# Two switch-expert stages: choice, gathering and combination rewritten

## The reference

```python
grouped = x.reshape(b, s // 32, 32, d)               # 64 groups of 32 tokens
logits = einsum('bntd,des->bntes', grouped, Wc) + bc  # 32 x 4 = 128 experts
logits = logits + tie                                 # 0 to 1e-6 over the 32 tokens
perm = (logits == max(logits, over the 32 tokens))    # one token per group and expert
permuted = einsum('bntd,bntes->bnesd', grouped, perm)
inner = relu(einsum('bnesd,esdf->bnesf', permuted, W1) + b1)   # 128 -> 32 features
result = einsum('bnesf,esdf->bnesd', inner, W2) + b2           # 32 -> 128
out = einsum('bnesd,bntes->bntd', result, perm)
```

## Time and profile before

| | us |
|---|---|
| median of 3 runs | 2787.95 |
| range of the runs | 2787.81 to 2790.35 |
| profiled execution | 2791.28 |
| its span, first to last instruction | 2789.5 |
| first switch stage in it | 2375.9 to 2473.5 |
| second switch stage in it | 2681.8 to 2780.3 |

### The profile page before, as it was taken

The page is one execution under the profiler, slowest core; times in us unless marked ns, Lnnn a source line. Parts: engine busy times, 40 slices in busy tenths (PEclk is TensorE's granted clock), DMA queues, the critical chain, the costliest instruction groups (busy, mean ns, idle before and its releaser), DMA issues. The chain is left out here.

```text
span 2789.5 us, 42839 instructions
## 1 busy us (share of the span) xinstructions
PE 2246.0 (81%) x15196; PEld 1529.7 (55%) x15196; DVE 1768.2 (63%) x4423; ACT 1388.1 (50%) x3630; POOL 718.1 (26%) x472
## 2 busy tenths in 40 slices
PE   5888887987988797897555888777776988689977
PEld 4666664663654464564335776243423766466647
DVE  5555555875964794794655664338355999447863
ACT  3444444763864584683621224554554765316750
POOL 0000001641640461461022431000010878041000
PEclk8999999989999998999767989798987999778986
DMA  1000002000100210110102320000001221100010
GB/s 54 13 13 13 13 1 73 21 20 19 24 17 5 81 25 12 24 28 4 47 9 54 74 53 18 11 11 3 6 11 33 87 72 53 64 10 1 2 64 16
DMA packets 79044, 80.94 MB, mean 29 GB/s; under 512 B 28624, under 2 KB 63952, under 8 KB 77808
## 3 DMA queue, kind: packets, MB, share of 16 engines
q1 hardware_dynamic: 78832, 78.19, 9.8%
HBM read 53.94 MB, written 8.52 MB: 22 GB/s over the span
## 5 line engine op out<-in xcount | busy, mean ns | idle before, releaser
L1016 ACT ACTIVATE window_s<-window_s,window_soft 128x128 f32<-128x128 f32 x512 | 197.8, 394 | 5.0 <-DVE window_soft L1179 5.0
L1094 POOL TENSOR_TENSOR window_pa<-window_pa,window_pb 128x1024 f32<-128x1024 f32 x64 | 151.5, 2366 | 152.3 <-DVE window_pb L1161 152.3
L1086 POOL TENSOR_TENSOR window_s<-window_s,window_soft 128x512 f32<-128x512 f32 x128 | 133.0, 1040 | 218.6 <-DVE window_soft L1116 218.4
L1179 DVE CUSTOM_DVE_ANT_0 window_s<-ps,window_mask,window_nrn 128x128 f32<-128x128 f32 x512 | 148.7, 347 | 46.7 <-PE ps L861 29.9
L3129 DVE TENSOR_TENSOR_SCAN mamba_bx<-ps,mamba_ab 128x256 f32<-128x256 f32 x256 | 154.6, 670 | 18.9 <-PE ps L2915 18.9
L824 PE MATMUL ps<-window_wa,window_sh 128*128 128x512 f32 x256 | 132.4, 643 | 41.6 <-DVE window_pb L1161 28.9
L417 PE MATMUL ps<-linattn_h,linattn_wb 128*128 128x512 f32 x192 | 107.5, 647 | 55.2 <-ACT linattn_h L494 55.2
L3299 ACT ACTIVATE rope_p<-ps,rope_mx 128x128 f32<-128x128 f32 (+1 forms) x256 | 104.3, 419 | 53.1 <-DVE rope_mx L3353 53.1
L2912 PE MATMUL ps<-mamba_m,mamba_xt 128*128 128x129 f32 x512 | 102.8, 283 | 29.6 <-ACT mamba_m L2987 20.6
L582 POOL TENSOR_TENSOR linattn_y<-linattn_y,linattn_wa 128x512 f32<-128x512 f32 x24 | 28.3, 1179 | 374.6 <-DVE linattn_xn L621 374.6
L83 PE MATMUL ps<-x,consts 128*128 128x512 f32 x120 | 78.4, 814 | 46.1 <-PEq L53 40.5
(11 more groups left out here) (607 smaller groups left out, 6243.3 us busy)
## 6 DMA issues: line engine op xcount, KB each, us to landing
mamba_cbr<-mamba_c SPq DMA_DIRECT2D x32, 512.0 KB, 3.6
window_vs<-window_vt SPq DMA_DIRECT2D x64, 128.0 KB, 2.3
delta_xi<-delta_x SPq DMA_DIRECT2D x16, 512.0 KB, 5.1
switch_w<-in_switch_w SPq DMA_DIRECT2D x4, 2048.0 KB, 10.0
window_wa<-in_window_wa SPq DMA_DIRECT2D x4, 1152.0 KB, 6.8
linattn_wb<-in_linattn_wb SPq DMA_DIRECT2D x6, 513.0 KB, 3.6
window_wb<-in_window_wb SPq DMA_DIRECT2D x4, 537.5 KB, 7.7
window_sh<-y SPq DMA_DIRECT2D x16, 128.0 KB, 2.2
```

Of the source, the lines that this page charges most:

```text
L1016: a = nc.scalar.activation(s[:, k % 2, e, c, :], s[:, k % 2, e, c, :], ACT.Exp, scale=-1.0, bias=soft[:, k % 2, e, 1, c:c + 1], accum_out= ...
L1086: nc.gpsimd.tensor_tensor(s[:, k % 2, e], s[:, k % 2, e], soft[:, k % 2, e, 3, :].unsqueeze(2).to_broadcast([P, QC, P]), ALU.mult)\
L1094: nc.gpsimd.tensor_tensor(own, own, pb[:, :, :, :].rearrange("p a h d -> p (a h d)"), ALU.add)\
L1179: v = nc.vector.tensor_tensor_reduce(s[:, k % 2, e, c, :], K.ps[:, B_S + e, toks(c, P)], mask[:, k % 2, :], nrn[:, k % 4, h:h + 1], 3e38, ...
```

## The change

- Choice: logits of chunk j go to bank 4 + j, the transposes of x to bank j. ACT's bias step is gone; DVE's first operation reads the logits from PSUM and adds bias and tie in one pass. ACT, not DVE, copies the transposed choice to `perm_tm`, and PE begins to gather after two chunks are turned.
- Gathering: a unit is a chunk and one of two pairs of groups (`units`). Its 8 products (16 passes) write two banks, j and j + 4; ACT copies the one, DVE the other, each with its own semaphore. `z` is laid out as feature, group, expert.
- Experts: the moving operand becomes `z[:, :, 4q + r]`, with steps of 128 words. `res` is a view of the same memory in the old order.
- Combination: the transposes of one chunk use banks 0 to 3; the copies to `resm` add nothing and are shared between ACT and DVE. For each tile a product of `perm` (128 tokens, stationary) with b2 (128 columns, moving) starts the sum; then each group's 32 columns of `perm` are the stationary operand on one of four column parts, and `resm`, 128 columns, moves. The result is tokens by features; ACT copies it to SBUF (`y_tm`, the memory of h), PE transposes it back, and DVE adds it to x. PE works on the transposes of chunk j + 1 ahead of the products of chunk j.

```diff
-    z = st.sb("z", [P, ES, NG])
+    z = st.sb("z", [P, NG, ES])
-    res = z
+    res = z[:, :, :].rearrange("p g e -> p (g e)").rearrange("p (e g) -> p e g", g=NG)
+    units = [(0, 0), (1, 0), (0, 1), (2, 0), (1, 1), (3, 0), (2, 1), (3, 1)]
+    seen = {u: n + 1 for n, u in enumerate(units)}
+    def picked_to(j, g):
+        return z[:, :, :].rearrange("p (j t g) e -> p j g t e", j=NJ, g=4)[:, j, g]
...
 PE
+            def turn_chosen(j):
+                pe.wait_ge(st.chosen, j + 1)
+                pe.wait_ge(st.x_copied, j + 1)
+                for t in range(TPW):
+                    mm = nc.tensor.transpose(K.ps[:, j, toks(t, P)], perm[:, toks(TPW * j + t, P)], K.ident)
+                mm.then_inc(st.chosen_tm, 1)
+            def pick(j, u):
+                pe.wait_ge(st.chosen_copied, j + 1)
+                if u:
+                    pe.wait_ge(st.picked_act, seen[j, 0])
+                    pe.wait_ge(st.picked_dve, seen[j, 0])
+                for t in range(TPW):
+                    for e in range(2):
+                        g = 2 * u + e
+                        rows, tile = slice(32 * g, 32 * g + 32), toks(TPW * j + t, P)
+                        mm = nc.tensor.matmul(K.ps[:, j + 4 * e, toks(t, P)], h_tm[rows, tile], perm_tm[rows, tile],
+                                              start=True, stop=True)
+                mm.then_inc(st.picked, 1)
+            def combine(j):
+                bank = K.ps[:, 4 + j % 2, :]
+                if j >= 2:
+                    pe.wait_ge(st.y_copied, j - 1)
+                for t in range(TPW):
+                    nc.tensor.matmul(bank[:, toks(t, P)], perm[:, toks(TPW * j + t, P)], b2, start=(t == 0), stop=False,
+                                     skip_group_check=True)
+                pe.wait_ge(st.moved_act, 2 * (j + 1))
+                pe.wait_ge(st.moved_dve, 2 * (j + 1))
+                for t in range(TPW):
+                    for g in range(4):
+                        n = 4 * (TPW * j + t) + g
+                        mm = nc.tensor.matmul(K.ps[32 * g:32 * g + 32, 4 + j % 2, toks(t, P)], perm[:, toks(n, GT)],
+                                              resm[:, n, :], start=False, stop=True, skip_group_check=True)
+                mm.then_inc(st.y_ready, 1)
...
+            for j in range(NJ):
+                logits(j)
+                turn_x(j)
+            turn_chosen(0)
+            turn_chosen(1)
+            for n, (j, u) in enumerate(units):
+                pick(j, u)
+                if n in (1, 3):
+                    turn_chosen(2 + n // 2)
...
-                                          z[:, 4 * q + r, :], start=True, stop=True)
+                                          z[:, :, 4 * q + r], start=True, stop=True)
...
-            for j in range(NJ):
-                pe.wait_ge(st.result_ready, min(4 * j + 4 + 8, NT))
-                for g in range(16 * j, 16 * j + 16):
-                    mm = nc.tensor.matmul(K.ps[:, 4 + j, toks(g % 16, GT)], resm[:, g, :], perm[:, toks(g, GT)],
-                                          start=True, stop=True)
-                mm.then_inc(st.y_ready, 1)
+            turn_result(0)
+            for j in range(NJ):
+                if j + 1 < NJ:
+                    turn_result(j + 1)
+                combine(j)
+                if j:
+                    turn_back(j - 1)
+            turn_back(NJ - 1)
...
 ACT
+            turned_chosen(0)
+            turned_chosen(1)
+            for n, (j, u) in enumerate(units):
+                picked(j, u)
+                if n in (1, 3):
+                    turned_chosen(2 + n // 2)
...
+            for j in range(NJ):
+                if j + 1 < NJ:
+                    moved(4 * j + 4)
+                    moved(4 * j + 6)
+                result(j)
...
 DVE
+                nc.vector.scalar_tensor_tensor(grouped(logit[:, toks(j)]), grouped(K.ps[:, 4 + j, :]), bc,
+                                               tie.unsqueeze(1).to_broadcast([P, 16, GT]), ALU.add, ALU.add)
...
+            choose(0)
+            choose(1)
+            choose(2)
+            picked(*units[0])
+            choose(3)
+            for j, u in units[1:]:
+                picked(j, u)
...
+            for j in range(NJ):
+                if j + 1 < NJ:
+                    moved(4 * j + 5)
+                    moved(4 * j + 7)
+                if j:
+                    attended(j - 1)
+            attended(NJ - 1)
```

More of the change, by code:

```diff
@@ new lines, in turn_result @@
+            def turn_result(j):
+                pe.wait_ge(st.h2_copied, ES // 8)
+                for n in range(4 * j, 4 * j + 4):
+                    if j:
+                        pe.wait_ge((st.moved_act, st.moved_dve)[n % 2], 2 * (j - 1) + n % 4 // 2 + 1)
+                    for g in range(4 * n, 4 * n + 4):
+                        mm = nc.tensor.transpose(K.ps[:, n % 4, toks(g % 4, P)], res[:, :, g], K.ident)
+                    mm.then_inc(st.turned, 1)
+            def combine(j):
[7 more added lines that the diff above has]
+                pe.wait_ge(st.moved_dve, 2 * (j + 1))
+                for t in range(TPW):
+                    for g in range(4):
[3 more added lines that the diff above has]
+                mm.then_inc(st.y_ready, 1)
@@ L3474, in _, with turn_back @@
+            def turn_back(j):
+                pe.wait_ge(st.y_copied, j + 1)
+                if j >= 2:
+                    pe.wait_ge(st.x_done, j - 1)
+                for t in range(TPW):
+                    mm = nc.tensor.transpose(K.ps[:, 6 + j % 2, toks(t, P)], y_tm[:, toks(TPW * j + t, P)], K.ident)
+                mm.then_inc(st.y_turned, 1)
             outer.pe(pe, 0, K.x, lambda j: None)
@@ L3476, in _ @@
             for j in range(NJ):
-                pe.wait_ge(outer.norm_ready, at(0, j))
-                nc.tensor.matmul(K.ps[:, j, :], wc, h[:, toks(j)], start=True, stop=True).then_inc(st.logit_ready, 1)
-            for j in range(NJ):
[L3480 to L3499, removed]
+                logits(j)
[6 more added lines that the diff above has]
+                    turn_chosen(2 + n // 2)
             pe.wait_ge(st.w2_ready, 32)
-            pe.wait_ge(st.picked_copied, NT)
+            pe.wait_ge(st.picked_act, 8)
+            pe.wait_ge(st.picked_dve, 8)
             for q in range(NQ):
@@ new lines, in turned_chosen, with moved, result @@
+            def turned_chosen(j):
+                act.wait_ge(st.chosen_tm, j + 1)
+                nc.scalar.activation(perm_tm[:, toks(j)], K.ps[:, j, :], ACT.Copy).then_inc(st.chosen_copied, 1)
+            def moved(n):
+                act.wait_ge(st.turned, n + 1)
+                nc.scalar.activation(resm[:, 4 * n:4 * n + 4, :], K.ps[:, n % 4, :].rearrange("p (g d) -> p g d", d=P),
+                                     ACT.Copy).then_inc(st.moved_act, 1)
+            def result(j):
+                act.wait_ge(st.y_ready, j + 1)
+                nc.scalar.activation(y_tm[:, toks(j)], K.ps[:, 4 + j % 2, :], ACT.Copy).then_inc(st.y_copied, 1)
@@ L3546, in _ @@
[L3546 to L3549 removed]
+                nc.scalar.activation(h_tm[:, toks(j)], K.ps[:, j, :], ACT.Copy).then_inc(st.x_copied, 1)
+            turned_chosen(0)
[4 more added lines that the diff above has]
+                    turned_chosen(2 + n // 2)
```

112 lines of the change are left out of this document (51 added, 61 removed).

## The result

The changed kernel takes 2740.94 us (median of 4 runs, 2740.1 to 2742.71) beside 2789.04 for the kernel before on the same chip (4 runs, 2787.81 to 2790.35): 0.9828 of the time, with an interval of 0.9811 to 0.9845. The two profiled executions took 2791.28 and 2740.96 us, a difference of 50.3; the prediction's terms are set against that.

A forecast was written before the change was run, and what follows sets the result against it. No engine was at its limit over the whole span, so two alike switch stages were priced: 2 x (11.0 + 0 + 14.2) + 2.2 = 52.6 us off the 2788.0 median gives 2735.4 us, range 2723 to 2764.

The forecast's parts named there:

- The sum: Whole kernel: 2 x (11.0 + 0 + 14.2) + 2.2 = 52.6 us saved, giving 2735.4 us on the median.
- Gathering, 11.0 a stage: Switch stage, choice to first expert product: start moves from 2415.56 to 2404.5, gain 11.0 us, bounds 6.4 and 14.9.
- First expert product, 0 a stage: L3504's product with moving columns 512 bytes apart: no change from 5.8 us; ends considered were 1.2 and 12.7 us more.
- own-path case: First expert product: each column part has its own read path, costing 1.2 us at 2.4 GHz and 0 at 1.2.
- (a): Rival, first expert product: four parts' strided reads share one path, +12.7 us per stage, total 2761 us; chance 0.20.
- (c): Rival, first expert product: no strided reads overlap, 145 ns a pass, +31.3 us per stage, total 2798 us; chance 0.04.
- a first product over 10 us: Sign that the forecast is wrong, pointing to (a) or (c); the forecast expected the first expert product to last 5 to 7.
- Second product, 0: Stretch from 2421.3 to 2437.0 us, with L3462's single-file copies untouched: left as it is, no gain.
- Combination, 22.3: Switch stage, first transpose to next stage's first product: 22.3 us for 36.5, gain 14.2, bounds 2.8 and 15.3.
- (b): Rival, combination: clock stays at 1.2 GHz, gain 2.8 us instead of 14.2, no 2.2 after, total 2760; chance 0.10.
- (d): Rival, combination: 32-column passes run one after another at 107 ns, +10.3 us per stage, total 2756 us; chance 0.03.
- After the stages, 2.2: After the switch stages: 1.5 us once in the rope's first passes and 0.7 us once in the store's transposes.

The follow-up runs named there:

- single-file run: Against the changed kernel, the gather copies wait for the other engine's last again, keeping their short contiguous stores; 2752.76 us in one run.

## Why the prediction was right, and the step that was wrong

**The sum.** 52.6 us were forecast off one execution and 50.3 came. The rest of the distance between 2735.4 and 2740.9 is the base: the forecast took the old execution to lie 3.3 us above the median, and the new one lies on its own (2740.96 and 2740.94). That the sum came so close is in part luck: the first product's miss of 9.7 us was paid back by 3.0 more in the gathering, 3.0 more after the stages and 1.05 and 1.1 that no term held. The stage, forecast at some 72 us, took 77.1 and 74.9.

**Gathering, 11.0 a stage: 10.3 and 14.7,** both between the bounds. Its first product was put at 2404.5 and started at 2404.14, in a stage that itself began 1.1 us earlier. The forecast took the first units slow and the rest fast, and neither stage did that. Stage 2 gathered at 1.00 throughout. Stage 1 did the reverse, the first two units fast and the other six at 1.2 GHz; there a unit took 1.5 us (6.07 for four), not the 1.9 forecast, and so two errors nearly cancelled. Copies and pairs came as priced.

**First expert product, 0 a stage: +4.83 and +4.92.** This is the step that failed: "I take 0, since most of L3504 ran at 1.2 GHz and the row is nearest to its own-path case". The mechanism that it chose was right, each part has its own path (one strided part costs nearly what four padded ones do), and rivals (a) and (c) are wrong: a pass took 47 to 37 ns, not 72 or 145. Still, the prediction's own sign against itself, a first product over 10 us, came true; it could not tell a third cause from those two. Two sizes were off. The price of a column, 1.13 ns, was that of a strided *stationary* load; a moving column on a line of its own costs 1.8 to 1.9. In the step's own formula that is 256 x (64 x 1.87 / 4 - 13.3) = 4.3 us at 2.4 GHz and 256 x (30 - 27) = 0.8 at 1.2, in place of 1.2 and 0. And the 512-byte step makes the paths hinder each other, 2.9 us more, of which no row of before could tell. A rise of the clock could give nothing back, since the pace did not depend on it.

**Second product, 0: -1.1 and 0.0.** Right as a term, but single-file copies left as they were hid some 6 us a stage, larger than the miss.

**Combination, 22.3: 22.55 and 22.54.** The first 16 transposes took 3.40 us as forecast, 32 products 1.08 us or, less the 0.22 of fill that the prediction took, 27 ns each; the granted clock was 1.00 from the second chunk on; rivals (b) and (d) are out. The bias passes were priced rightly at 0.86 a chunk; what was not asked is whether DVE could have carried the bias for less, and it can, by 3.5 us a stage.

The Trainium skill, "TensorE: Matmul & The Clock Gate", section "Part 4: PE-mode transpose", holds that transposes don't count as busy to the clock gate. As before the change, the trace disagrees: within L3498's transposes, after 3.40 us at a mean of 0.54, the granted clock stood at 1.00.

**After the stages, 2.2: 3.3 in the rope and 1.9 in the store.** The direction was right, and so was the reason for the rope: its first 8 passes took 3.67 us for 5.90. But that stage's code never changed, and it took 201.8, 205 to 206 or 208 us among these kernels, by how long the granted clock stood at 0.50 within it: 17.1 us in the kernels with 201.8, 27.3 with 205 to 206, 30.7 or more with 208, where before had 31.8. In the run with one strided part, which left its switch stage with the new combination, the clock fell 0.9 us into the rope stage for 3.4 us, and the stage took 208.0. What decides this stays open, and the forecast had no term for it.

Open as well: why a pass at the 512-byte step falls from 47 to 37 ns in the course of the product, and why a moving column on its own line costs 1.8 ns and a stationary one 1.13. A single strided part with another step was not tried, so its 1.8 ns may hold something of the 512 bytes. That four padded parts come to 1.9 leaves little room for it.

## What to carry to other kernels

Where a change moves a strided access from one side of a copy to the other, price it on the reader too, and by a row of the same kind of operand: here each gather copy became 0.3 to 0.4 us shorter and the product that reads them lost 4.9 us a stage. Lay out fp32 for TensorE's moving operand so that two columns share 16 bytes, or at least off a step of 512 bytes; only the second was timed in several runs here. And look at the waits next to the change: copies that alternate between two engines through one counter cost more here than the whole miss, and the group's "idle before" column named them.

## What the runs showed of the hardware

- A pass of 64 fp32 columns on four 32-column parts takes 15 ns at steps of 8 bytes and 2.4 GHz, 30 at 16 or 528, and 47 to 37 at 512, the last three whatever the clock.
- ACT and DVE storing words 256 bytes apart slow each other when both begin at the same moment. With the operand laid out by expert again, most pairs did in stage 1, and the copies took 1294 and 1256 ns for 1034 and 1016 in single file. In stage 2 most began a few tenths of a us apart and, though they overlapped, took 1.02 to 1.13 us; the last pair began together, with PE idle, and took 1.30 and 1.29:

```profile
L3569 ACT ACTIVATE switch_z<-ps 128x512 f32<-128x512 f32 x8 | 8.2, 1096 | 1.8 <-PE ps L3488 1.8
L3629 DVE COPY switch_z<-ps 128x512 f32<-128x512 f32 x8 | 7.8, 1076 | 0.5 <-PE ps L3488 0.5
```

```profile
2676.78 1.30 ACT L3569 ACTIVATE switch_z<-ps 128x512 f32<-128x512 f32 x1 [0.70 <-PE ps L3488]
2676.78 1.29 DVE L3629 COPY switch_z<-ps 128x512 f32<-128x512 f32 x1 [0.46 <-PE ps L3488]
```

- DVE's first addition beside a product with four parts at 512 bytes took 1.03 us (L3653 at 2407.68) and 1.15 in stage 2; the later ones took 0.69, and all did with steps of 8, 16 or 528 bytes, with contiguous columns, and with only one or two parts by steps. In the other kernels with four parts at 512 bytes the first one took 0.70 to 1.80 us, longest in stage 2 of the single-file run, whose product was also the slowest (11.4 us). So DVE is slow just where this product is slowest; that the product's reads hinder it is likely, but was not tried by itself.
